# Moving the rows of q and k in column sets, with their parts made as a pipeline and the values projected among the first maxima

## The reference, cut to what matters

```
def _L3_conv_ref(x, q_w, k_w, v_w):          # q_w, k_w: 16 x 64, v_w: 64 x 64
    xf = x.reshape(b, din, hw)               # hw = 3136
    Q = jnp.einsum('kc,bcp->bkp', q_w, xf)
    K = jnp.einsum('kc,bcp->bkp', k_w, xf)
    V = jnp.einsum('vc,bcp->bvp', v_w, xf)
    S = jnp.einsum('bkp,bkq->bpq', Q, K)
    A = jax.nn.softmax(S, axis=-1)
    z = jnp.einsum('bpq,bvq->bvp', A, V)
    return z.reshape(b, V.shape[1], h, w)
...
x = x + _L3_conv_ref(_gn(x), L3_conv_q_w, L3_conv_k_w, L3_conv_v_w)
```

## Time and profile before

| | us |
|---|---|
| median of 3 runs | 1942.02 |
| lowest and highest | 1940.48, 1942.21 |
| the profiled execution's own time | 1941.18 |
| its span, first to last instruction | 1939.4 |
| PE busy | 1673.0 (86%) |
| DVE busy | 1257.6 (65%) |
| ACT busy | 1250.2 (64%) |
| POOL busy | 1098.9 (57%) |
| mean granted TensorE clock | 0.92 of 2.4 GHz |

### The profile page before, as it was taken

One profiled execution on the slowest core, in us unless ns is written; L12 is line 12 of the kernel. 1 busy time (PEld: TensorE's weight loads), 2 busy tenths in 40 slices (PEclk: granted clock), 3 DMA queues, 4 the chain that ended last, 5 costly groups with the idle time before them and its releaser, 6 DMA issues.

```text
span 1939.4 us, 35957 instructions
## 1 busy us (share of the span) xinstructions
PE 1673.0 (86%) x10840; PEld 829.7 (43%) x10840; DVE 1257.6 (65%) x2446; ACT 1250.2 (64%) x2324; POOL 1098.9 (57%) x898
## 2 busy tenths in 40 slices
PE   5885899999887689999987859999999776999997
PEld 4362344444436234444443624444444452444442
DVE  5845777776574667777467466777748636777770
ACT  2035788888413578888831348888872335888885
POOL 3610477778651057777865006777787301677777
PEclk9996799999888689999998859999999796999998
DMA  2004000000000400000000040000000021000000
GB/s 81 0 1 83 1 7 6 6 6 6 12 0 1 83 1 6 6 6 6 11 7 1 2 82 2 6 6 6 11 6 5 0 32 19 1 6 11 6 6 10
DMA packets 8568, 26.91 MB, mean 14 GB/s; under 512 B 2256, under 2 KB 5840, under 8 KB 7888
## 3 DMA queue, kind: packets, MB, share of 16 engines
q1 hardware_dynamic: 8400, 24.79, 5.5%
HBM read 8.73 MB, written 6.42 MB: 8 GB/s over the span
## 4 chain that ended last, share of the span: by engine, by line
PE 50%; issue 16%; DVE 12%; POOL 10%; ACT 7%; SPq 3%; DMA 1%; POOLq 1%; ACTq 0%; DVEq 0%
PE PS L1202 20%; PE PS L1126 10%; PE PS L1158 9%; DVE nmt L642 4%; ACT PS L819 3%; SPq L369 3%; ACT Pb L862 2%; DVE nmt L635 2%; POOL accP L971 2%; POOL VT L928 2%; POOL VT L933 2%; POOL VT L930 2%; PE PS L1023 2%; PE PS L1111 2%; PE PS L1098 1%
## 5 line engine op out<-in xcount | busy, mean ns | idle before, releaser
L635 DVE TENSOR_REDUCE nmt<-PS 128x1 f32<-128x448 f32 x1176 | 680.3, 620 | 282.2 <-PE PS L1126 277.9
L971 POOL TENSOR_TENSOR accP<-accP,Pb 128x512 f32<-128x512 f32 (+1 forms) x532 | 677.9, 1274 | 167.3 <-ACT Pb L862 143.6
L862 ACT ACTIVATE Pb<-PS 128x896 f32<-128x896 f32 (+1 forms) x700 | 638.9, 914 | 132.0 <-PE PS L1158 107.1
L1202 PE MATMUL PS<-Pb,VT 128*64 128x448 f32 x2800 | 657.1, 549 | 4.4 <-ACT Pb L862 3.6
L1126 PE MATMUL PS<-Ka,Qa 96*64 96x448 bf16 x2744 | 514.2, 388 | 119.1 <-DMA Ka<-parts 57.7
L1158 PE MATMUL PS<-Qa,Ka 99*64 99x448 bf16 x2744 | 490.0, 358 | 5.3 <-ACT Qa L834 4.0
L819 ACT ACTIVATE PS<-PS,nmt 128x448 f32<-128x448 f32 x588 | 356.4, 606 | 120.0 <-DVE nmt L642 92.6
L1126 PEld LDWEIGHTS PS<-Ka,Qa 96*64 96x64 bf16 x2744 | 164.1, 115 | 421.7 <-issue 163.4
L1158 PEld LDWEIGHTS PS<-Qa,Ka 99*64 99x64 bf16 x2744 | 162.4, 111 | 249.5 <-issue 184.9
L1202 PEld LDWEIGHTS PS<-Pb,VT 128*64 128x64 f32 x2800 | 191.7, 138 | 95.7 <-ACT Pb L862 23.7
L964 POOL TENSOR_TENSOR accQ<-Pb 128x512 f32<-128x512 f32 x28 | 35.6, 1270 | 292.6 <-ACT Pb L862 292.6
(11 more groups left out here) (141 smaller groups left out, 1416.3 us busy)
## 6 DMA issues: line engine op xcount, KB each, us to landing
xin<-in_x SPq DMA_DIRECT2D x4, 1568.0 KB, 6.9
out<-xw SPq DMA_DIRECT2D x28, 224.0 KB, 1.9
Qa<-parts SPq DMA_DIRECT2D x48, 98.0 KB, 3.9
Ka<-parts SPq DMA_DIRECT2D x48, 98.0 KB, 4.1
wz<-in_weights SPq DMA_DIRECT2D x1, 829.0 KB, 8.2
cs<-in_cst SPq DMA_DIRECT2D x1, 576.0 KB, 8.8
wz<-in_weights SPq DMA_DIRECT2D x1, 576.0 KB, 9.6
cs<-in_cst SPq DMA_DIRECT2D x1, 256.0 KB, 6.3
```

Source lines behind the costliest of these rows:

```text
L635: nc.vector.reduce_max(nmt[:, target % 2, b, t:t + 1], PS[0:BLK, bank, 0:CH], X, negate=True).then_inc(mx_free, 1)
L862: nc.scalar.activation(Pb[0:r, j % PSLOTS, :, :], PS[0:r, 2 * (k % 2):2 * (k % 2) + 2, 0:CH], ACT.Exp).then_inc(exp_done, 1)
L971: nc.gpsimd.tensor_tensor((accQ if j < TO_ACCP else accP)[0:r, :, REST:CH], (accQ if j <= TO_ACCP else accP)[0:r, :, REST:CH], Pb[0:r, j % ...
L1202: last = mm(PS[C * h:C * h + C, OB, 0:CH], VT[:, j, C * h:C * h + C], Pb[:, j % PSLOTS, h, :], start=(j == 0), stop=(j == NQ - 1))
```

## The change

Four things change in the opening and the first maxima; the superblocks and the three other layers stay.

1. The columns of `qk3` are laid out anew, so that the two images' rows of q, and of k, alternate. One transfer moves 16 rows of both images (from 32 partitions to 16 partitions by 2), and columns can be chosen. A group has 24 transfers as before, now four sets of six: the first chunk of q (448 columns), the first three chunks of k (1344), the other four chunks of k (1792), the other six chunks of q (2688). Each set has a semaphore of its own.
2. ACT and DVE make the parts as a pipeline: ACT's order is normalise chunk j, high part of j - 1, middle part of j - 2; DVE's is rest of j, low part of j - 1.
3. The first maxima go through the key chunks one after another (`FIRST_ORDER`, seven tiles to a key chunk, of which tiles 0, 2 and 4 are summed), so the first 21 tiles need three chunks of k and one of q.
4. The values are projected among the first maxima: after the fourth tile of each seven, PE projects four blocks of 128 positions into bank 7, and ACT copies them after the last tile of the seven. PE waits for the copy of one before it projects the next.

```diff
-SPREADS = 12
+SPREADS = 6
+FIRST_KEYS = 3
...
+def order_first():
+
+    blocks = [b for b in range(ACT_BLOCKS, NJ)]
+    summed = {m * NJ // ACT_BLOCKS: m for m in range(ACT_BLOCKS)}
+    row = [summed[n] if n in summed else blocks.pop(0) for n in range(NJ)]
+    return [(b, t) for t in range(NJ) for b in row]
+
+
+FIRST_ORDER = order_first()
...
+            def spread(dst, part, c0, c1, loaded):
+
+                base, order = (0, Q_ORDER) if dst is Qa else (2 * DK, K_ORDER)
+                for r in range(KROWS // DK):
+                    if order[r] == part:
+                        sp.dma_start(dst[DK * r:DK * r + DK, :, c0:c1],
+                                     parts[base:base + 2 * DK, part, c0:c1]).then_inc(loaded, 16)
...
             def group(g, last):
+                sp.wait_ge(part_h, NJ * g + 1)
+                spread(Qa, 0, 0, CH, q_first)
+                sp.wait_ge(part_m, NJ * g + 1)
+                spread(Qa, 1, 0, CH, q_first)
+                sp.wait_ge(part_h, NJ * g + FIRST_KEYS)
+                spread(Ka, 0, 0, FIRST_KEYS * CH, k_first)
+                sp.wait_ge(part_l, NJ * g + 1)
+                spread(Qa, 2, 0, CH, q_first)
+                sp.wait_ge(part_m, NJ * g + FIRST_KEYS)
+                spread(Ka, 1, 0, FIRST_KEYS * CH, k_first)
+                sp.wait_ge(part_l, NJ * g + FIRST_KEYS)
+                spread(Ka, 2, 0, FIRST_KEYS * CH, k_first)
                 for part, ready in enumerate((part_h, part_m, part_l)):
                     sp.wait_ge(ready, NJ * g + NJ)
-                    for h in range(2):
-                        spread(part, h)
+                    spread(Ka, part, FIRST_KEYS * CH, HW, k_rest)
+                for part in range(3):
+                    spread(Qa, part, CH, HW, q_rest)
...
-                for j in range(NJ):
-                    low_part(dve, g, j)
+                    if j:
+                        low_part(dve, g, j - 1)
+                low_part(dve, g, NJ - 1)
...
+                for j in range(NJ + 2):
+                    if j < NJ:
+                        normalise_chunk(rows(xnf[:, j * CH:(j + 1) * CH]), xw, j, xn_ready[3])
+                    if 1 <= j <= NJ:
+                        high_part(j - 1)
+                    if j >= 2:
+                        middle_part(j - 2)
...
+                    if b == NJ - 1:
+                        value_part(t)
...
+                def value_columns(i):
+
+                    if i:
+                        pe.wait_ge(v_ready, NJ * g + i)
+                    for j in range(4 * i, min(4 * i + 4, NQ)):
+                        r = key_rows(j)
+                        last = mm(PS[0:r, 7, (j % 4) * P:(j % 4 + 1) * P], xnf[:, j * QC:j * QC + r], wcol("wv3"),
+                                  start=True, stop=True)
+                    last.then_inc(v_ps, 1)
...
-                pe.wait_ge(v_ready, NJ * (g + 1))
-                for loaded in qk_loaded:
-                    pe.wait_ge(loaded, 16 * (SPREADS * (g + 1) + 1))
-                for i in range(TILES):
...
+                pe.wait_ge(q_first, 16 * (SPREADS * (g + 1) + 1))
+                pe.wait_ge(k_first, 16 * (SPREADS * (g + 1) + 1))
+                for i in range(TILES):
+                    b, t = FIRST_ORDER[i]
+                    if i < NJ:
+                        pe.wait_ge(rest_h, NJ * g + i + 1)
+                    elif FIRST_ORDER[i - NJ][0] < ACT_BLOCKS:
+                        pe.wait_ge(first_summed, ACT_TILES * g + sum(b < ACT_BLOCKS for b, _ in FIRST_ORDER[:i - NJ + 1]))
+                    else:
+                        pe.wait_ge(first_used, TILES * g + i - NJ + 1)
+                    if i == FIRST_KEYS * NJ:
+                        pe.wait_ge(k_rest, 16 * (SPREADS * (g + 1) + 1))
+                    tile_of(i % NJ, 0, b, t).then_inc(first_ready, 1)
+                    if i % NJ == NJ // 2:
+                        value_columns(i // NJ)
+                pe.wait_ge(v_ready, NJ * (g + 1))
                 max_rows(NJ * g, 7)
                 pe.wait_ge(mrow, NJ * g + 1)
+                pe.wait_ge(q_rest, 16 * (SPREADS * (g + 1) + 1))
```

More of the change, by code:

```diff
@@ L315, in build @@
         part_l = sem("qk_part_low")
-        qk_loaded = [sem(f"qk_rows_loaded_{h}") for h in range(2)]
+        q_first = sem("first_q_columns_loaded")
+        k_first = sem("first_k_columns_loaded")
+        k_rest = sem("other_k_columns_loaded")
+        q_rest = sem("other_q_columns_loaded")
         first_ready = sem("first_max_scores_ready")
@@ L357, in _ @@
             sp.sem_inc(stored, 16)
-            for loaded in qk_loaded:
+            for loaded in (q_first, k_first, k_rest, q_rest):
                 sp.sem_inc(loaded, 16)
@@ L361, in _ @@
                 sp.sem_inc(first, 1)
[L363 to L370, removed]
+            Q_ORDER, K_ORDER = (0, 0, 1, 0, 2, 1), (0, 1, 0, 2, 0, 1)
+            def spread(dst, part, c0, c1, loaded):
[4 more added lines that the diff above has]
+                                     parts[base:base + 2 * DK, part, c0:c1]).then_inc(loaded, 16)
             def store(g):
@@ L791, in group, with high_part @@
                     normalise_chunk(padded(dst, j), xw, j, done)
-                act.wait_ge(gn_nb[3], g + 1)
-                for j in range(NJ):
-                    normalise_chunk(rows(xnf[:, j * CH:(j + 1) * CH]), xw, j, xn_ready[3])
+                def high_part(j):
+                    act.wait_ge(qk_ps, NJ * g + j + 1)
+                    nc.scalar.activation(parts[:, 0, j * CH:(j + 1) * CH], PS[0:4 * DK, j, 0:CH],
+                                         ACT.Copy).then_inc(part_h, 1)
                 def middle_part(j):
@@ L799, in middle_part, with value_part @@
                                          ACT.Copy).then_inc(part_m, 1)
[L801 to L810, removed]
+                act.wait_ge(gn_nb[3], g + 1)
+                for loaded in (q_first, k_first, k_rest, q_rest):
+                    act.wait_ge(loaded, 16 * (SPREADS * g + 1))
+                for j in range(NJ + 2):
[5 more added lines that the diff above has]
+                        middle_part(j - 2)
+                def value_part(i):
                     m = min(4, NQ - 4 * i)
@@ L814, in group @@
                     nc.scalar.activation(VT[0:r, 4 * i:4 * i + m, :],
-                                         PS[0:r, i, 0:m * P].rearrange("p (a b) -> p a b", b=P),
+                                         PS[0:r, 7, 0:m * P].rearrange("p (a b) -> p a b", b=P),
                                          ACT.Copy).then_inc(v_ready, 1)
@@ L879, in group @@
                 for i in range(TILES):
-                    b, t = ORDER[i]
+                    b, t = FIRST_ORDER[i]
                     if b < ACT_BLOCKS:
@@ L1112, in group, with tile_of @@
                        start=True, stop=True).then_inc(qk_ps, 1)
[L1113 to L1124, removed]
+                def value_columns(i):
[6 more added lines that the diff above has]
+                    last.then_inc(v_ps, 1)
+                def tile_of(bank, s, b, t):
                     for h in range(2):
@@ L1143, in max_tile @@
                     wait_bank(last)
-                    tile_of(bank, target, i).then_inc(mx_ready, 1)
+                    tile_of(bank, target, *ORDER[i]).then_inc(mx_ready, 1)
                 def max_rows(sidx, bank):
@@ L1309 @@
         put("wq", a["L1_conv_Wq"], C * h, CR * h)
-        put("qk3", a["L3_conv_q_w"].T, 2 * DK * h, C * h)
-        put("qk3", a["L3_conv_k_w"].T, 2 * DK * h + DK, C * h)
+        q_col, k_col = COLS["qk3"][0], COLS["qk3"][0] + 2 * DK
+        arrays["weights"][C * h:C * h + C, q_col + h:q_col + 2 * DK:2] = a["L3_conv_q_w"].T
+        arrays["weights"][C * h:C * h + C, k_col + h:k_col + 2 * DK:2] = a["L3_conv_k_w"].T
         put("wv3", a["L3_conv_v_w"].T, C * h, C * h)
```

1 line of the change is left out of this document (removed).

## The result

The changed kernel takes 1880.54 us in the median of 4 runs (1877.83 to 1881.19) against 1942.05 before: a ratio of 0.9684, 95% interval 0.9672 to 0.9696. The profiled execution took 1879.96 us, with a span of 1878.2 and a mean clock of 0.95. One execution in this document is left out of what is read from the times: 3899 us, of the kernel of `e6`, whose four others took 1876 to 1878.

A forecast was written before the change was run, and what follows sets the result against it. The serial opening behind SP's transfer queue was taken as the bound, with DVE pacing the tiles behind it. A gain of 14.4 less 2.3 us for values, four times, is 48.4 us: forecast 1894 us, range 1879 to 1910.

The forecast's parts named there:

- the case that I gave 62%: Whole kernel: the main forecast of 1894 us, with its own range of 1885 to 1903 us.
- the rest of the kernel: Behind the first maxima: no term in the sum, which counted only opening and values, 4 x (14.4 - 2.3) us.
- the signs that I named: Profile after: first reduction 14 to 15.5 us after `xnf` starts, 49 tiles in 27 to 30 us, among others.
- The first tile: Opening of each group: DVE's first tile at 164.0 against 179.06 us in group 0, counted as 14.4 us a group.
- the landing: Last of the first twelve transfers: issued at 159.4, landing the median 4.0 us later, at 163.4 us.
- its lower bound: Opening: smaller transfers could land after 2.9 us, and then low part 6 gates, 0.5 us sooner.
- The rest of q: Last transfers of a group: landed by 174 us, asked for after the 49th tile, so hidden.
- by the piece: Rival on transfers: twice the pieces make the first twelve take as long as 24 did; 1929 us, chance 7%.
- The values' cost: Values among the first maxima: 2.3 us a group, bounds 0 and 5.2.
- I expect a change to and fro, half the rows slow: PE's clock under the tiles: alternates between 1.2 and 2.4 GHz, 3 x 0.87 = 2.6 us, taken as 2.3 a group.
- The ring: Value projection waits for ACT's copy, behind its sums: 3.5 us a row at 2.4 GHz, 4.6 at 1.2, against DVE's 3.73.
- all is hidden: Rival: clock rises and stays, last early transfer lands after 2.9 us, low part 6 gates; 1882 us, chance 12%.

The follow-up runs named there:

- e6: Changed kernel with each value matmul done twice and ACT's copy of the values ahead of the row's third sum: 1876.23 us, 1876.86 in a second run.
- e8: Kernel of e10 with the low parts made by POOL in place of DVE: 1876.06 us.
- e4: Changed kernel without column sets, 12 transfers a group of both images and all 3136 columns: 1970.57 us, ratio 1.0147 to the kernel before.
- e7: Changed kernel with one key chunk in the first set of k in place of three: 1906.68 us.
- e1: Kernel before the change with only the values moved among the first maxima: 1944.96 us, ratio 1.0019.
- e3: Changed kernel with the parts made one kind after another, without the pipeline: 1902.85 us.
- e10: Changed kernel with ACT's copy of the values ahead of the row's third sum, values projected once: 1875.54 us, ratio 0.9667 to the kernel before.
- e9: Changed kernel with serial parts and values ahead of the tiles, so column sets and tile order alone: 1890.61 us.
- e2: Changed kernel with the values projected ahead of the tiles again, between the projection of q and k and the first tile: 1899.22 us.
- e5: Changed kernel with each value matmul of the tile stage done twice: 1890.70 us.

## Why the prediction was right, and where it was off

**The bound was read rightly.** The opening was a serial piece behind SP's queue, and its gain shows one to one: -60.9 of the 61.2 us of span.

**The number** is inside the range, but only near its lower end, and the case that I gave 62% (1885 to 1903) didn't come: 13.5 us less than my 1894. About 3 of them are the first tiles, 7 the values, 3 the rest of the kernel; all three errors point the same way. Two of the signs that I named were missed on the same side: the first reduction 13.8 us after ACT starts `xnf` (14 to 15.5 named), and the tiles in 26.5 to 26.9 us (27 to 30 named).

**The first tile** was forecast 14.4 us a group sooner and came 15.2 sooner. The parts came as worked out: rounds of 1.55 us on ACT, the last low part 14.3 us after `nb` in place of 13.3. The term that was off is the landing, taken as 4.0 us, the median of transfers of 98 KB. The last of the first twelve is issued at 160.17, lands 2.5 us later, and PE starts at 162.74. With that DVE's low part was the gate, as the text had it for its lower bound, and `e8` shows by how much: with the low parts on POOL the first reduction comes 0.6 us sooner and then waits for PE.

**Why cutting columns works** was put wrongly in one place: "landing times of 2.9 to 5.4 didn't grow along the queue as a backlog's would". `e4` and `e7` show that the size of what is queued does count: 2352 KB take 20.3 us in 24 transfers and 22.4 in 12, and landing times do grow along the queue where large transfers follow one another (3.9 to 11.9 us in `e4`, 3.2 to 8.8 over the last twelve of the changed kernel). The first two sets are 6 x 28 + 6 x 84 = 672 KB of this. I counted issues at 0.63 us, which fitted for these: they are issued 0.63 us apart where no part is waited for, and land in 1.9 to 2.9 us without a growth. The rest of q, forecast to have landed by 174, landed at 177.6, still long before it is asked for. The rival "by the piece" is excluded all the same: the changed kernel has twice the pieces of before (768 in a group), and all have landed 24.6 us after the first issue (153.03 to 177.62), where by the piece it would be 40.6.

**The values' cost** was the larger error: 2.3 us a group forecast, 0.5 measured, of which 0.3 to 0.6 is the one wait of DVE shown above. The step that failed is "I expect a change to and fro, half the rows slow". The clock was at 1.00 when the tiles began, at 0.50 for 3 us, and at 0.99 over the next 17, in which PE was busy 12.9 us. In `e1`, `e3` and `e4`, where the stage begins after a long idle stretch, the slow part is one row and costs 1.5 us. The pipeline's part in this wasn't in the sum: it keeps PE at work until shortly before the tiles. The rule of the Trainium skill that I weighed (TensorE: Matmul & The Clock Gate, "A second HAM failure mode: psum-queue depth-cycling") fits rows 8 only in part: there, with tiles alone, the clock rose once, for about 3 us (1.00 over 659.0 to 662.4), fell back, and stayed at 1.2 GHz for the rest of the stage (0.50 over 662.4 to 681.9). I read a to and fro out of one rise. With the values in the stage the clock fell once and rose once, and didn't oscillate; there the measurement decides.

**The ring** is real and was sized about right: 3.5 us by my sum at 2.4 GHz against 3.73 of DVE, and 4.33 measured with 0.9 more of values. At 1.2 GHz my sum was 4.6, and the slow row of the changed kernel's group 0 took 4.34 (values at 167.71 and again at 172.05). `e10` takes away all that was left of the values' cost, but not by the ring alone: with the early copy the granted clock stays at 1.00 through the tiles of all four groups, so no row is slow. How much of the 0.5 us was the ring and how much PE's own work at 1.2 GHz isn't shown.

**The rest of the kernel** I had at zero; it gave 2.7 us. This is no instruction of the change. Over the experiments the same instructions took 1563.0 to 1569.5 us, and it goes with the clock in the first 15 us behind the split. Group 1 of the changed kernel against its group 0:

```profile
190.40:205.40 15.00, 12.54 (x79) 5.72 (x81) 6.83 (x19) 10.02 (x19) 6.14 (x5) 0.72 0.01 2
651.40:666.40 15.00, 12.56 (x67) 5.50 (x69) 5.39 (x14) 8.56 (x16) 4.65 (x4) 0.62 0.01 2
```

The sum of the four clocks in such windows is 2.85 in `e9` (rest 1563.0), 2.76 after the change (1565.3), 2.67 before (1568.0), 2.64 in `e3` (1569.2) and 2.59 in `e2` (1569.5). The nearest to a test is the second profile of the changed kernel, where the same groups drew other clocks: group 0 had 0.66 and took 422.7 us from the split to the next `nb` (0.72 and 419.9 in the first profile), group 1 had 0.71 and took 420.4 (0.62 and 422.8). That the clock is the cause is argued from this order, not shown by an edit. Of the rivals, "all is hidden" (1882 us, 12%) came nearest; I gave it too little.

## What to carry to other kernels

When a stage waits for data that are moved in one piece, move first what the first steps need and order the steps by it; what is saved is the wait for the bytes that the first step doesn't need, and a first set that is too small (`e7`) brings a second wait. Edits around one gap should be tried together as well as alone: the pipeline and the moved values lost 9 and 12 us singly and won 10 as a pair. When work is slipped into a stage that another engine paces, look for the ring of waits it closes, and put the copy that frees the buffer ahead of work that waits for something else.

## What the runs showed of the hardware that I had not expected

- Twelve transfers of 196 KB between two places of the on-chip memory had 9.0 us to landing in the median and up to 11.9, while SP issued one every 0.96 us; 24 of 98 KB had 4.0. The time for the same 2352 KB was 22.4 and 20.3 us.
- With tiles alone the clock was at 1.2 GHz through the stage (`e9`, from 170 to 193 us: 0.50, PE busy 18.4 of 23 us); with the values among them, and PE busy 12.9 of 17 us, it stayed at 2.4. Which property of the work decides, the runs don't tell. In each group of the changed kernel the clock was down once, for about 3 us; with the values doubled (`e5`) or copied earlier (`e10`) it didn't fall among the tiles.
- The time from the split of the maxima to a high clock differs between groups of one execution, and over the kernels here the time of the same instructions behind the split, 1563.0 to 1569.5 us in all, goes with it.
